# Second self-attention: both head parities in one item, all turns written out, and GpSimd making the repeated bf16 terms of queries and keys

## The reference, cut to what matters

```python
x_norm = x * jax.lax.rsqrt(jnp.mean(x * x, axis=-1, keepdims=True) + EPS) * w_norm
qkv = bit_linear(x_norm, w_qkv)          # activations rounded to 8 bits, weights to -1, 0, 1
q = q.reshape(b, s, NH, HD)...           # 32 query heads, 8 key/value heads, head size 8
q = apply_rotary(q, cos, sin)
k = apply_rotary(k, cos, sin)
scores = jnp.einsum('bkgsd,bktd->bkgst', qg, k) / np.sqrt(HD)
scores = jnp.where(causal[None, None, None, :, :], scores, -jnp.inf)
attn = jax.nn.softmax(scores, axis=-1)
out = jnp.einsum('bkgst,bktd->bkgsd', attn, v)
return bit_linear(out, w_out)
```

## Time and profile before

| | |
|---|---|
| time, median of 3 runs | 3753.85 us (3726.41 to 3762.97) |
| the profiled execution | 3760.45 us, span 3758.7 us |
| busy over the whole span | PE 82%, DVE 51%, ACT 41%, POOL 31% |
| granted clock, mean | 0.822 |
| the stage that is changed | 2034 to 2727 us |

### The profile page before, as it was taken

The page is one execution under the profiler, slowest core; times in us unless marked ns, Lnnn a source line. Parts: engine busy times, 40 slices in busy tenths (PEclk is TensorE's granted clock), DMA queues, the critical chain, the costliest instruction groups (busy, mean ns, idle before and its releaser), DMA issues. The chain is left out here.

```text
span 3758.7 us, 50944 instructions
## 1 busy us (share of the span) xinstructions
PE 3073.0 (82%) x13981; PEld 1795.9 (48%) x13983; DVE 1924.6 (51%) x4543; ACT 1550.5 (41%) x3160; POOL 1177.8 (31%) x1058
## 2 busy tenths in 40 slices
PE   5799999879999768788794799999957742888884
PEld 2477777557777534444353333333234411355553
DVE  5666666756666567777614455554232340223323
ACT  3555555545555347777511233332225410023331
POOL 1477777367777400000001000000010027044443
PEclk8899999989999855555597589887759965699997
DMA  1122121021111073000000000000000024077885
GB/s 57 46 53 52 35 50 19 12 79 35 51 51 35 23 231 107 1 1 0 27 0 16 0 1 1 1 0 0 1 20 1 0 85 145 9 161 163 182 178 122
DMA packets 127085, 192.73 MB, mean 51 GB/s; under 512 B 17552, under 2 KB 88208, under 8 KB 125584
## 3 DMA queue, kind: packets, MB, share of 16 engines
q1 hardware_dynamic: 83696, 134.71, 12.7%
q0 software_dynamic: 23616, 33.24, 5.0%
q10 hardware_dynamic: 19584, 22.57, 2.2%
HBM read 123.23 MB, written 67.25 MB: 51 GB/s over the span
## 5 line engine op out<-in xcount | busy, mean ns | idle before, releaser
L228 DVE SCALAR_TENSOR_TENSOR h_pre<-h_px,h_par,h_pre 128x510 f32<-128x510 f32 (+2 forms) x384 | 286.5, 746 | 271.3 <-ACT h_pre L689 251.4
L843 POOL TENSOR_TENSOR norm_rstd<-norm_mv,mhalf 128x4 f32<-128x4 f32 x24 | 28.2, 1177 | 1134.9 <-DVE norm_mv L826 1134.9
L652 PE MATMUL h_po<-h_wo,h_h 128*128 128x256 f32 x1024 | 329.9, 413 | 0.0
L2921 POOL DMA_INDIRECT moe_sums<-ex_y,ex_sidx x132 | 204.8, 1552 | 321.0 <-DVE ex_y L3089 304.1
L574 POOL TENSOR_SCALAR h_decay<-h_cumb,h_sel 128x256 f32<-128x256 f32 x256 | 291.6, 1139 | 25.3 <-DMA h_cumb<-cum_rows 25.3
L585 POOL TENSOR_TENSOR h_mix<-h_decay,cb 128x768 f32<-128x768 f32 x128 | 232.9, 1819 | 167.1 <-ACT h_decay L675 167.1
L616 PE MATMUL h_px<-x_cols,h_w 128*128 128x512 f32 x512 | 254.4, 620 | 25.4 <-DMA h_d<-d_skip 25.4
L2038 DVE TENSOR_REDUCE at_nmax<-at_pd 128x2 f32<-128x512 f32 (+1 forms) x192 | 132.5, 690 | 258.9 <-PE at_pd L1772 256.7
L621 PE MATMUL h_pz<-x_cols,h_w 128*128 128x512 f32 x512 | 241.7, 594 | 6.3 <-DVE h_gate L742 6.3
L1256 ACT ACTIVATE xq_ex<-xq_ps,xq_nmax,xq_qs 128x512 f32<-128x512 f32 x256 | 199.4, 779 | 113.6 <-DVE xq_nmax L1324 113.2
L1921 ACT ACTIVATE at_ex<-at_ps 128x512 f32<-128x512 f32 x192 | 114.5, 597 | 291.3 <-PE at_ps L1798 159.7
(11 more groups left out here) (397 smaller groups left out, 6498.6 us busy)
## 6 DMA issues: line engine op xcount, KB each, us to landing
h_cumb<-cum_rows SPq DMA_DIRECT2D x32, 1024.0 KB, 8.4
moe_tiles<-blank SPq DMA_DIRECT2D x4, 6642.0 KB, 44.1
ex_w<-moe_w SPq DMA_DIRECT2D x64, 352.0 KB
ex_xg<-moe_tiles ACTq DMA_DIRECT2D x136, 162.0 KB
ex_wd<-moe_wd SPq DMA_DIRECT2D x64, 176.0 KB
h_w<-w_xg SPq DMA_DIRECT2D x8, 1024.0 KB, 10.4
moe_sums<-blank SPq DMA_DIRECT2D x2, 2176.0 KB, 26.7
h_wo<-w_out SPq DMA_DIRECT2D x8, 512.0 KB, 10.3
```

The lines of the kernel that those rows point to most:

```text
L228: ins = dve.scalar_tensor_tensor(out=out[:, :, back:S], in0=src[:, :, 0:S - back], scalar=par[:, at + CK - 1 - back:at + CK - back], in1=o ...
L652: pe.matmul(po[t // TPB][:, t % TPB, :], hh[j % 2][:, t * P:(t + 1) * P], w_out[s.pg][:, j, :], start=(j == 0 and t % TPB == 0), stop=(j = ...
L2921: pool.indirect_dma_start(out=r.sums[i % 2][:, :], out_offset=bass.IndirectOffsetOnAxis(ap=sidx[i][:, 0:1], axis=0), in_=y[i % 2][:], in_o ...
```

## The change

Scores: an item (`item(d)`, 12 per batch) holds both parities of a group of heads, eight heads for the first token tile, four for the second. `pd` now has two banks, one for each parity. The matmuls over 48 rows come first, parity by parity in alternation, and then two identity matmuls add the mask to all heads of a bank.

Transposed scores: 12 items of both parities, with one `ps` of two banks where two single ones stood. Three items make a group, whose exponentials lie in one of two buffers `ex`; `mix` comes once per group and runs all four column groups of `po` together. `po` is single now.

GpSimd makes the repeated terms (`double`, new), after `split` and before the new semaphore `doubled`, on which `pturn` waits. The key casts write both halves of the keys' row at once, and splits cover both token tiles in one instruction. The copies of `po` to `mT` and of the values move to ScalarE; `vt` is gone, `val` and `kT` have three buffers. The maxima are split once per batch instead of twice.

Order: a turn has 24 slots. Each step stands at a number (`at`) counted from the batch's own start, `due` tells which batch is at that step in a slot, and all turns from -1 to 9 are written out, without a hardware loop. The quantisation saves one small instruction (the factor 127).

```diff
+        SLOTS = 24
+        SPLIT, TURNS = (14, 18), (17, 19, 19, 20, 21, 22)
+        SCORE, MSPLIT, QTURNS, TSCORE = 24, 47, (49, 50, 51, 52), 55
+        MIX, MTURN, DIVIDE = 60, 62, 64
...
+            def double(s, kind):
+
+                pool.wait_ge(split, s * 2 + kind + 1)
+                for dst, src in (KCOPIES if kind else QCOPIES):
+                    if kind:
+                        for u in range(TPB):
+                            ins = pool.tensor_copy(kp[:, u, :, :, AD * dst:AD * (dst + 1)], kp[:, u, :, :, AD * src:AD * (src + 1)])
+                    else:
+                        ins = pool.tensor_copy(qp[s % 2][:, :, :, AD * dst:AD * (dst + 1)], qp[s % 2][:, :, :, AD * src:AD * (src + 1)])
+                ins.then_inc(doubled, 1)
...
-                for i, h in enumerate(heads):
-                    lo = 64 * (h % 2)
-                    pe.matmul(pd[:, i * keys:(i + 1) * keys], qT[s.par][lo:lo + PD, h // 2, u * P:(u + 1) * P],
-                              kT[s.par][lo:lo + PD, h // AG, 0:keys], start=True, stop=False)
-                    mm = pe.matmul(pd[:, (i + 1) * keys - P:(i + 1) * keys], r.identb[:], causal[:],
-                                   start=False, stop=True)
+                after(pe, topped, s * ND + d)
+                for i in range(ni):
+                    for par in range(2):
+                        h, lo = head + 2 * i + par, 64 * par
+                        pe.matmul(pd[:, par, i * keys:(i + 1) * keys], qT[s % 2][lo:lo + PD, h // 2, u * P:(u + 1) * P],
+                                  kT[s % 3][lo:lo + PD, h // AG, 0:keys], start=(i == 0), stop=False, skip_group_check=True)
+                for par in range(2):
+                    view = pd[:, par, :].rearrange("p (i k) -> p i k", k=keys)
+                    mm = pe.matmul(view[:, :, keys - P:keys], r.identb[:], causal[:, None, :].to_broadcast([P, ni, P]),
+                                   start=False, stop=True, skip_group_check=True)
...
+            def mix(s, n):
+                pe.wait_ge(expd, s * ND + (n + 1) * GD)
...
+                for j in range(2):
+                    for par in range(2):
+                        at = VW * (j * 2 + par)
+                        pe.matmul(po[at:at + VW, :, :], val[s % 3][:, 0, 2 * n + j, :], ex[n % 2][:, j, par, :].rearrange("p (i t) -> p i t", i=2),
+                                  start=True, stop=False, skip_group_check=True)
...
-                dve.tensor_reduce(nmax[:, u, heads[0]:heads[-1] + 1:2], pd[:].rearrange("p (h k) -> p h k", k=P * (u + 1)),
+                best = nmax[:, u, head:head + 2 * ni].rearrange("p (i q) -> p q i", q=2)
+                dve.tensor_reduce(best, pd[:].rearrange("p q (i k) -> p q i k", k=P * (u + 1)),
                                   AX.X, ALU.max, negate=True).then_inc(topped, 1)
```

More of the change, by code:

```diff
@@ L1552, in bit_quant, with after @@
     return dve.tensor_scalar(xi, x, ROUND, None, ALU.subtract)
-def deep_turns(eng, body):
-    def turn(b, par):
-        return [Batch(b + k, (par + k) % 2) if not isinstance(b, int) or 0 <= b + k < B else None for k in (-2, -1, 0, 1)]
-    for b in range(3):
-        body(*turn(b, b % 2))
-    with eng.Fori(0, (B - 4) // 2) as i:
-        body(*turn(i * 2 + 3, 1))
-        body(*turn(i * 2 + 4, 0))
-    for b in range(B - 1, B + 1):
-        body(*turn(b, b % 2))
+def after(eng, sem, count):
+    if count > 0:
+        eng.wait_ge(sem, count)
 def attn1_tokens(nc, a, r, wqkv, wout, wscale):
@@ L1641, in attn1_tokens @@
         split = sem("split")
+        doubled = sem("doubled")
         pturned = sem("pturned")
@@ L1745, in pturn @@
                 kind, u, half = BANKS[n]
[L1746 removed]
+                pe.wait_ge(doubled, s * 2 + (1 if kind == "q" else 2))
                 if n < 2:
[L1749 to L1750 removed]
+                    pe.wait_ge(valued, s + 1)
+                    after(pe, (okept, added)[n], s - 2)
                 else:
[L1752 removed]
+                    pe.wait_ge(pkept, s * NB + n - 1)
                 bank = pab[n % 2][:].bitcast(BF16)
@@ new lines, in qturn @@
+            def qturn(s, n):
+                u, half = divmod(n, 2)
+                pe.wait_ge(msplit, s + 1)
+                pe.wait_ge(pkept, min(s + 2, B) * NB)
+                if n >= 2:
+                    pe.wait_ge(qkept, s * NQ + n - 1)
+                bank = pab[half][:].bitcast(BF16)
+                for j in range(8):
+                    at = 16 * half + 2 * j
+                    mm = pe.transpose(bank[:, j * P:(j + 1) * P], qp[s % 2][:, u, at:at + 2, :].rearrange("p a c -> p (a c)"), r.identb[:])
+                mm.then_inc(qturned, 1)
@@ L2035, in top @@
-            def top(s, m):
-                dve.wait_ge(scored, LEAD + s.b * NI + m + 1)
-                u, heads = maxima[m]
-                dve.tensor_reduce(nmax[:, u, heads[0]:heads[-1] + 1:2], pd[:].rearrange("p (h k) -> p h k", k=P * (u + 1)),
+                    src = rot[:, :, AH:AH + AKV, :]
+                    parts, order = [kp[:, :, :, :, AD * n:AD * (n + 1)] for n in range(PARTS)], KORDER
+                    after(dve, pturned, s * NB)
+                else:
+                    src, parts, order = rot[:, :, 0:AH, :], [qp[s % 2][:, :, :, AD * n:AD * (n + 1)] for n in range(PARTS)], QORDER
+                    after(dve, qturned, (s - 1) * NQ)
@@ L2039, in top, with maxsplit @@
+                thirds(src, [parts[at] for at in order]).then_inc(split, 1)
+            def top(s, d):
+                u, head, ni = item(d)
+                dve.wait_ge(scored, s * ND + d + 1)
+                best = nmax[:, u, head:head + 2 * ni].rearrange("p (i q) -> p q i", q=2)
+                dve.tensor_reduce(best, pd[:].rearrange("p q (i k) -> p q i k", k=P * (u + 1)),
                                   AX.X, ALU.max, negate=True).then_inc(topped, 1)
-            def maxsplit(s, u):
+            def maxsplit(s):
```

483 lines of the change are left out of this document (216 added, 267 removed).

## The result

The changed kernel takes 3489.18 us (median of 4 runs, 3479.48 to 3490.39), the kernel before 3757.23 us beside it (4 runs, 3726.41 to 3762.97). The ratio is 0.9296, with a 95% interval of 0.9243 to 0.935: 7.0% faster, 268 us. The forecast was 3534 us, 220 us less than before, with a range of 3470 to 3610.

A forecast was written before the change was run, and what follows sets the result against it. TensorE was taken to bound the seven full turns before the change. Full turns -192 us, turn 0 -27, the end -3, the start +2: -220, giving 3540 for the profiled execution and 3534 for the median, range 3470 to 3610.

The forecast's parts named there:

- Steps (1) to (3): TensorE's scores, transposed scores and value products per batch at full clock: 8.8, 8.8 and 5.7 us after the change.
- 0.66 and 0.89: TensorE's us per score or transposed-score item of the second and first kind, with row pairs side by side.
- 1.42: TensorE's us for one group of value products, four column groups running together; four such groups take 5.7.
- rival A: Row pairs on TensorE do not run side by side: 5.3 us more per turn, 3571 us in all; chance 0.10.
- I take the middle, 51: Length in us of a full turn, between 43 at full clock and 60 at half; seven turns 549 to 357.
- Rival C: TensorE's clock stays low because it rests in each item: all full turns take 60 us, 3597 in all; chance 0.13.
- 2.5 us for handovers: Allowance added to a full turn for products waiting on the last exponential and similar handovers.
- laid-out sum of 40.5: Larger of TensorE's and VectorE's work between scores, summed over items 0 to 11 of a full turn at full clock.
- Step (6): GpSimd's nine copies, taken as 1.0 and 0.4 us each, hidden behind TensorE's items but for 0.2 us per batch.
- B: GpSimd's copies are late or hold up VectorE: 6 us per batch, 3582 us in all; chance 0.14.
- D: Slower than before, each batch waiting for GpSimd's copies in runs of eight elements, needing 17 ns each; chance 0.03.
- Rival B's second part: VectorE's two-input subtractions beside GpSimd's copies are held up by about their own length, 2 us per batch.

The follow-up runs named there:

- experiment 1: Kernel before, with one part of the change alone: masks added once per score item, behind all its small-row matmuls; 3664.17 us against 3738.07, ratio 0.9799.
- experiment 9: Changed kernel, each parity's small-row matmuls followed by their own mask, in scores and transposed scores; 3478.26 us against the changed kernel's 3417.83 in its series.
- experiment 3: Changed kernel, with VectorE making each reduction of the scores twice; 3580.37 us, ratio 0.9581 to the kernel before.
- experiment 10: Kernel before and changed kernel run once more without edit; changed kernel's ratio to the kernel before 0.9325.
- experiment 4: Changed kernel, with the first query transpose one slot later (17 to 18); 3479.58 us, ratio 0.9307 to the kernel before.
- 11: Changed kernel, first query transpose and the output's transpose and projection one slot later, residual add ahead of the splits; 3396.88 us, ratio 0.927 to the kernel before.
- 5: Changed kernel, small-row matmuls within an item written one parity after the other, masks still together; 3412.24 us, ratio 0.9325 to the kernel before.
- 7: Changed kernel, values' products written column group by column group, 512 columns then 256 of each; 3412.57 us, ratio 0.9332 to the kernel before.

## Why the forecast was right in kind and 45 us off

**Steps (1) to (3), TensorE, held.** The change costs 0.10 us (experiment 1), pairs in different row groups run side by side (0.33 us for four matmuls of 256 columns, and 4.7 us of a turn in experiment 9), and four column groups run together (0.88 us). The items priced at 0.66 and 0.89 and the values' 1.42 stand within some 0.03 us in the timeline. So rival A falls, by trace and by experiment. The Trainium skill's rule (TensorEngine Tiling (Array Packing), Key Properties), that different tiles work in parallel, agrees with these rows. Of the 32 us that a turn lost, the order of sizes is the values' products (20.2 to 5.7 us by the terms; no run undoes them alone), the masks together (9 with the clock's part, experiment 1) and the row pairs with the two changes per item that they save (4.7, experiment 9). These prices add up only while TensorE is the bound. Not tested alone either are the copies of `po` on ScalarE and the written-out turns.

**The term that was mis-sized is "I take the middle, 51".** The turn at full clock was worked out as 43 us, and turns of 43.1 us were measured, 302 us for seven instead of 357. That one term is 55 us; the other stretches took 4 us more than forecast (120 against 116), so the stage as a whole is 51 below its forecast. The clock was expected to fall since TensorE would rest more; it stood at 0.88 to 1.00 from the second full turn on, mean 0.93 in the turns with all steps, and experiment 3 has 0.81 to 0.88 with TensorE busy for about 70% of the turn. The prediction's own two ends, 43 us at full clock and 60 at half, give some 45 us at 0.93 (an estimate, on the straight line between them). So about 6 of the 8 us per turn are the level of the clock, and 2 the sum for full clock, which was too long.

Rival C falls with it. Its likeness to turn 0 was close, and still misled: in the earlier trace rows turn 0 stood at 0.50 with TensorE busy for 71% of it and waiting at most 1.9 us for VectorE at a time; the turns of experiment 3 have as large a busy share and waits of up to 2.0 us, at 0.81 to 0.88. The waits, in turn 0 of the kernel before (2069 to 2132 us) and in experiment 3 (2163 to 2440 us):

```profile
PE at_pd L1770 <- DVE at_nmax L2038: 15.3, 18, 1.9
```

```profile
PE at_pd L1780 <- DVE at_nmax L2057: 43.8, 35, 2.0
```

That the clock has a price is seen in the first full turn: 43.2 us at 0.68 and 40.3 at 0.79 (experiment 10), and 37.6 at 0.91 in experiment 4, whose moved transpose takes off some of that. Between 0.88 and 0.96 the turns with all steps show no such order (43.2 us at 0.88, 44.1 at 0.92). Why the clock holds in one pattern and not in the other these runs do not settle; turn 0 also comes out of a start at half clock, and no run took the two apart.

**That 43 was met exactly is partly luck.** It holds 2.5 us for handovers and 0.2 for GpSimd. TensorE waited 2.1 us per turn for the query copies and 1.4 for the residual add. Without all or most of them (experiments 4 and 11) the turn is 41.4 and 41.2, at a mean clock of 0.95 and 0.94, not 1.0. So the laid-out sum of 40.5 was good, and the allowance was 1 us, not 2.5. The measured 43 is made of that smaller allowance, the waits behind GpSimd and the residual add, and a clock a little under full.

**Step (6), "hidden but for 0.2", was wrong for a reason other than the length.** The copies are shorter than taken (0.617 and 0.293 for 1.0 and 0.4 us). What was overrated is the cover. The timelines of VectorE and GpSimd in one turn:

```profile
2219.51 0.43 DVE L2028 CAST at_qp<-at_rot 128x512 bf16<-128x512 f32 x1
2220.03 1.23 DVE L2053 TENSOR_REDUCE at_nmax<-at_pd 128x4 f32<-128x1024 f32 x1
...
2225.87 0.29 DVE L2028 CAST at_kp<-at_rot 128x256 bf16<-128x256 f32 x1
2226.30 0.88 DVE L2088 SCALAR_TENSOR_TENSOR x_rows<-at_pab,at_oamax,x_rows 128x256 f32<-128x256 f32 x2
2230.26 1.22 DVE L2053 TENSOR_REDUCE at_nmax<-at_pd 128x4 f32<-128x1024 f32 x1 [3.08 <-PE at_pd L1783]
```

```profile
2220.00 1.72 POOL L1719 COPY at_qp<-at_qp 128x512 bf16<-128x512 bf16 x3 [23.58 <-DVE at_qp L2028]
2226.23 1.47 POOL L1717 COPY at_kp<-at_kp 128x128 bf16<-128x128 bf16 x6 [4.50 <-DVE at_kp L2028]
```

The split ends at 2219.94 us and the copies at 2221.72, while TensorE had run out of items 1.52 us before it could start the transposes at 2221.78. I had counted TensorE's items between the slots as cover and left out that VectorE reaches the end of the split later than TensorE reaches those items: the split itself takes VectorE 3.0 us (2216.97 to 2219.94), and in that time TensorE works off what was to cover the copies. TensorE's wait for GpSimd, 2.1 us per turn, is over the 1 us that the prediction gave as a sign of B or D, and neither is its cause. Then the second transposes wait for the residual add, which stands behind the key split. At 2230.26 the delay comes back to VectorE as an idle 3.08 us.

**Rival B's second part, the hold-up of VectorE, exists but hardly ever acts.** At the start of the stage the key split runs beside GpSimd's query copies:

```profile
2059.38 0.68 DVE L2028 CAST at_kp<-at_rot 128x256 bf16<-128x256 f32 x1
2060.13 0.54 DVE L2031 TENSOR_TENSOR at_rot<-at_rot,at_kp 128x128 f32<-128x128 f32 x1
...
2061.73 0.29 DVE L2028 CAST at_kp<-at_rot 128x256 bf16<-128x256 f32 x1
2059.30 1.84 POOL L1719 COPY at_qp<-at_qp 128x512 bf16<-128x512 bf16 x3 [12.46 <-DVE at_qp L2028]
```

The cast takes 0.68 us and the subtraction 0.54 in place of 0.29, and once GpSimd has stopped they are back at 0.29. In the full turns the two splits stand four slots apart, and the reduction beside the copies (2220.03) keeps its 1.23 us. The Trainium skill's rule (SBUF — State Buffer, Who interferes with whom) on a two-input VectorE instruction agrees for the subtraction. It costs about a microsecond in the whole stage, not 2 per batch.

**Smaller terms.** Turn 0: forecast 36, measured 37. Start: forecast 37, measured 35. VectorE per turn: forecast 31 us busy, measured 31 to 32; its share came to 73% instead of 65 because the turn is shorter. ScalarE: 26 to 29 forecast, 25 to 27 measured; reductions 1.22 forecast and measured. The end was to take 43 us and took 48, at a clock of 0.68: the last batch has nothing beside it, and the change takes no instruction out of its output.

## What to carry to other kernels

Read the price of a change of tile shape on TensorE from start-to-start distances, count the changes, and first group what has one shape: that gave some 9 of the 32 us that a full turn lost, in four lines. Price a wait on a helper engine from the moment its input is ready on the engine ahead of it, and not from the slots between; a move of small copies to a slower helper engine can be worth next to nothing even when it frees the busiest partner (here 1 us of 43). Before a wait is removed, ask which engine comes last behind it: here more than half of the first wait's time, and three quarters of the next ones', came back as a wait for VectorE. Do not let a clock level be decided by analogy with one stretch of the trace: here that guess outweighed all the other errors, and one run with an artificially slowed partner would have measured it.

## What the runs showed of the hardware that was not expected

- The order in which matmuls of one shape are written within a run of them does not decide whether they overlap: written one row group after the other, or one column group after the other, they took the same 0.33 and 0.88 us (experiments 5 and 7). What ended the overlap was a full-row matmul between them (experiment 9).
- Four fp32 products of 512 columns in four column groups take 0.88 us, as long as one alone (0.98 less the change).
- The granted clock stood at 0.81 to 0.88 in turns with TensorE busy for about 70% (experiment 3), and at 0.50 in turns 0 with 45% (experiment 3) and with 71% (the kernel before).
- A one-input VectorE cast, too, took 0.68 in place of 0.29 us beside a GpSimd copy.
- Strided bf16 copies in runs of eight elements: 0.617 us on GpSimd and 0.289 on VectorE for 512 elements per partition, 0.293 and 0.188 for 128.
